# Four attention layers on one core: replicated bias rows, an epsilon tile, and a place of its own for every step of every group

## What is computed

```python
def _L0_xattn_ref(query, key, Wq, bq, Wk, bk, Wv, bv, Wo, bo):     # and the same once more as L3
    Q = query @ Wq + bq; K = key @ Wk + bk; V = key @ Wv + bv
    weights = softmax(Q @ K.T * scale)
    return query + (weights @ V) @ Wo + bo
def _L1_xattn_ref(text, audio, video, ...):                        # audio = ctx, video = side
    out_a, out_v = _cma(text, audio, ...), _cma(text, video, ...)  # layer norms, then attention
    output = out_a + out_v + text
    return _ln(output, ln_g, ln_b) @ fc_W + fc_b + output
def _L2_xattn_ref(emb, latent, ...):
    w = softmax(q @ k.T * scale, axis=1)                           # over the queries
    x = w @ v + emb
    return (x - mu) * rsqrt(var + EPS) * gamma + beta
```

## Time and profile before

| what | value |
|---|---|
| median of 3 runs | 614.36 us (613.43 to 615.67) |
| the profiled execution, its time | 613.34 us |
| its span in the trace | 611.5 us |
| mean granted clock of PE | 0.993 of full speed |
| PE busy, instructions | 582.3 us (95%), 4872 |
| DVE busy | 537.5 us (88%) |
| POOL busy | 520.0 us (85%) |
| ACT busy | 431.5 us (71%) |

### The profile page before, as it was taken

How to read it: one execution, slowest core, us unless ns; L and a number is a source line. 1 busy time by engine, 2 the same in 40 slices (tenths; PEclk the granted TensorE clock), 3 DMA queues, 4 the chain that set the end, 5 groups by cost and what they waited for, 6 DMA issues and landing times. The chain is left out here.

```text
span 611.5 us, 16892 instructions
## 1 busy us (share of the span) xinstructions
PE 582.3 (95%) x4872; PEld 567.7 (93%) x4872; DVE 537.5 (88%) x1685; ACT 431.5 (71%) x1473; POOL 520.0 (85%) x694
## 2 busy tenths in 40 slices
PE   4889999899999999999999999999999999999985
PEld 4778999899999999999999999999999899999974
DVE  1457789999999999999999999999999999989993
ACT  2546967777777778778777777877876788677443
POOL 3268887898999999999999999999999999867763
PEclk9998999999999999999999999999999999999999
DMA  8512211003222211122222221112333020000012
GB/s 274 217 62 70 82 48 46 3 1 96 80 78 80 78 56 51 54 80 79 78 80 79 79 79 53 48 60 78 114 104 114 17 89 28 18 3 19 19 35 70
DMA packets 28076, 42.80 MB, mean 70 GB/s; under 512 B 2513, under 2 KB 19793, under 8 KB 27985
## 3 DMA queue, kind: packets, MB, share of 16 engines
q1 hardware_dynamic: 27986, 41.72, 20.6%
HBM read 33.32 MB, written 8.39 MB: 68 GB/s over the span
## 5 line engine op out<-in xcount | busy, mean ns | idle before, releaser
L720 ACT ACTIVATE prob_L<-bank,neg_max_L 128x128 f32<-128x128 f32 x320 | 114.1, 379 | 70.1 <-DVE neg_max_L L952 69.7
L1082 POOL TENSOR_SCALAR xhat_ln<-x,rstd_ln,shift_ln 128x256 f32<-128x256 f32 x128 | 71.1, 564 | 14.0 <-issue 7.4
L652 ACT ACTIVATE oT_hi_L<-bank 128x256 fp32r<-128x256 f32 (+1 forms) x128 | 55.9, 460 | 34.4 <-PE bank L476 34.4
L720 ACT ACTIVATION_READ_ACCUMULATOR prob_L<-bank,neg_max_L 128x1 f32 x320 | 69.1, 216 | 0.0
L952 DVE TENSOR_REDUCE neg_max_L<-bank 128x2 f32<-128x256 f32 (+1 forms) x128 | 59.0, 477 | 11.5 <-PE bank L470 11.1
L652 ACT ACTIVATE xT_hi_L<-bank 128x512 fp32r<-128x512 f32 (+1 forms) x96 | 59.5, 620 | 7.4 <-PE bank L448 7.1
L854 DVE TENSOR_TENSOR oT_lo_L<-bank,oT_hi_L 128x256 fp32r<-128x256 f32 (+1 forms) x128 | 58.7, 478 | 2.9 <-ACT oT_hi_L L652 2.8
L1076 POOL TENSOR_TENSOR rstd_ln<-var_eps_ln,minus_half 128x2 f32<-128x2 f32 x64 | 45.3, 708 | 12.6 <-DVE var_eps_ln L919 7.4
L1116 POOL TENSOR_TENSOR xT_lo_L<-x_in,xT_hi_L 128x512 fp32r<-128x512 f32 x32 | 41.0, 1282 | 12.2 <-ACT xT_hi_L L652 12.2
L652 ACT ACTIVATE probT_L<-bank 128x256 f32<-128x256 f32 (+1 forms) x96 | 47.4, 495 | 4.3 <-PE bank L454 4.1
L985 DVE TENSOR_TENSOR x<-bank,x_bias 128x512 f32<-128x512 f32 x64 | 43.8, 685 | 6.5 <-PE bank L489 4.3
(11 more groups left out here) (217 smaller groups left out, 2390.9 us busy)
## 6 DMA issues: line engine op xcount, KB each, us to landing
x_in<-in_x SPq DMA_DIRECT2D x32, 512.0 KB, 4.2
ctx_in<-in_ctx SPq DMA_DIRECT2D x32, 256.0 KB, 4.3
out<-y SPq DMA_DIRECT2D x32, 256.0 KB, 2.2
side_in<-in_side SPq DMA_DIRECT2D x32, 128.0 KB, 2.5
WqT_L<-in_L_WqT SPq DMA_DIRECT2D x3, 256.0 KB, 4.3
Wo_L<-in_L_Wo SPq DMA_DIRECT2D x2, 256.0 KB, 4.7
WkT_L<-in_L_WkT SPq DMA_DIRECT2D x3, 128.0 KB, 4.1
WvT_L<-in_L_WvT SPq DMA_DIRECT2D x2, 128.0 KB, 4.0
```

The costliest lines, as they stand in the source:

```text
L652: activation(to, of, ACT.Copy).then_inc(done[step], 1)
L720: last = activation(at(prob[k], g)[:, b, :], block(bank, b), ACT.Exp, bias=at(neg_max[k], g)[:, b:b + 1], accum_out=at(total[k], g)[:, b:b ...
L1082: last = pool.tensor_scalar(at(to, g)[:, n, :], tile, at(rstd[k], g)[:, n:n + 1], at(shift[k], g)[:, n:n + 1], ALU.mult, ALU.add)
```

## The change

Four things.

1. The biases that were added on PE by a product of a row of ones with a bias row (`ones_row`, `row`) are gone. Ten rows of weights (`L0_bo`, `L1a_bo`, `L1v_bo`, `L3_bo`, `L3_b1`, `fc_bias`, `L2_bv`, `L3_g1` and the two key gains) are loaded by DMAs that write one row to all 128 partitions. They are added on DVE (`bias_plus`, which takes the place of an ACT copy) or multiplied in on POOL (`gained_L1a`, `gained_L1v`).
2. `var_eps` is a `tensor_tensor` with a tile `epsilon` in the place of a `tensor_scalar` with a number.
3. The preparations are cut into single steps (`M_L0`, `N_L0`, `m_L0`, ...), each with a place in the table, and the weights come in smaller loads with a semaphore each (`load_qk_`, `load_vo_`).
4. The table `STARTS` holds a number for every step and every group, 32 in a row, in the place of one pattern and the shifts `COMES`.

```diff
-STARTS = {"load_x": 0, "hi_L0": 107, "lo_L0": 281, "load_ctx": 580, "Q_L0": 626, "hi_ctx": 640, "q_L0": 727,
...
+    "rstd_keys": [2220, 2626, 2725, 4293, 5070, 6321, 7384, 8075, 8327, 12940, 13236, 15067, 16634, 17974, 20211, 21563, 23380,
...
-    table = [(STARTS[name] + COMES[g], g, name) for name in STARTS for g in range(GROUPS)]
...
+    table = [(times[g], g, name) for name, times in STARTS.items() for g in range(GROUPS)]
...
-        ones_row = sb("ones_row", [1, P])
...
+        epsilon = {e: sb(f"epsilon_{i}", [P, 2 * GROUP]) for i, e in enumerate((EPS_L1, EPS_L2))}
...
+            def replicated(to, r, what):
+                n, width = ROWS.index(r), to.shape[1]
+                sp.dma_start(to[:], ins["rows"][n:n + 1, 0:width].to_broadcast([P, width])).then_inc(weights[what], 16)
+
+            def load_qk(a):
+                return lambda: two(a, "WqT", "WkT", "qk")
...
-                dve.tensor_scalar(at(var_eps[k], g)[:], mv[:, :, 1], eps, None, ALU.add).then_inc(done[f"var_{k}"], 1)
+                if g == 0:
+                    prepared(dve, "constants")
+                dve.tensor_tensor(at(var_eps[k], g)[:], mv[:, :, 1], epsilon[eps][:, 0:len(tiles)], ALU.add).then_inc(done[f"var_{k}"], 1)
...
+            def bias_plus(key, to, use, added):
+                dve.tensor_tensor(to[:], bank_of(use)[:, 0:D], added[:], ALU.add).then_inc(done[key], 1)
...
+            def gained(a):
+                def of():
+                    pool.wait_ge(weights[f"{a}_qk"], TWO)
+                    pool.wait_ge(weights[f"gain_{a}"], ONE)
+                    w = stage[a]["WkT"]
+                    pool.tensor_tensor(w[:], w[:], gain[a][:].unsqueeze(1).to_broadcast([P, T, P]), ALU.mult).then_inc(done[f"gained_{a}"], 1)
+                return of
```

More of the change, by code:

```diff
@@ L61 @@
+PREPARATIONS = {"M_L0": 395, "N_L0": 615, "m_L0": 484, "n_L0": 528, "M_L1a": 1027, "N_L1a": 2128, "m_L1a": 1205, "M_L1v": 1116, "N_L1v":
[11 rows of a table added]
+COPIES = {"x_in": 3, "x_bias": 3, "x2_bias": 2, "token_sums": 2, "x3_bias": 2, "ctx_in": 10, "side_in": 3, "keys": 3, "keysT": 2,
[9 rows of a table added]
 SCALE = float(D) ** -0.5
@@ L77 @@
               "S_L3": "exp_L3", "PT_L3": "pT_L3", "O_L3": "oT_lo_L3", "OUT_L3": "out_L3"}
[L79 to L87, removed]
@@ L88 @@
-SMALL = [f"{what}_{k}" for what in ("stats", "mean", "var") for k in ("keys", "ln1", "lnf", "ln2")] + ["x_gamma"]
-SIGNALS = {"TensorE": {"keys_L1": ["gain_L1a", "gain_L1v"], "products_L0": ["M_L0", "N_L0"], "vectors_L0": ["m_L0", "n_L0"],
[13 rows of a table removed]
+EMPTIED_BY |= {"m_L0": "m_col_L0", "n_L0": "bias_L0", "m_L1a": "m_col_L1a", "m_L1v": "m_col_L1v", "n_L1": "bias_L1", "n_fc": "bias_fc",
+               "mean_fc": "centred_fc", "M_L2": "M_lo_L2", "k_L2": "k_bias2", "m_L3": "m_col_L3", "n_L3": "bias_L3"}
+EMPTIED_BY |= {f"{w}_{a}": f"{w}_lo_{a}" for w in "MN" for a in ATTENTIONS}
@@ new lines @@
+OF_ENGINE = {"TensorE": [f"{w}_{a}" for w in "MNm" for a in ATTENTIONS] + ["n_L0", "n_L1", "n_L3", "n_fc", "mean_fc", "M_L2", "k_L2"],
+             "ScalarE": ([f"{w}_hi_{a}" for w in "MN" for a in ATTENTIONS] + [f"M0_{a}" for a in ("L1a", "L1v", "L3")]
+                         + ["N0_L1a", "N0_L1v", "gained_fc", "F_hi", "M_hi_L2", "Wv2_hi"]),
+             "VectorE": (["scaled"] + [f"{w}_lo_{a}" for w in "MN" for a in ATTENTIONS] + [f"m_col_{a}" for a in ATTENTIONS]
+                         + ["bias_L0", "bias_L1", "bias_L3", "bias_fc", "centred_fc", "F_lo", "M_lo_L2", "k_bias2", "Wv2_lo"]),
+             "GpSimd": ["constants", "gained_L1a", "gained_L1v", "rows_L1", "rows_L3"] + [f"rep_{a}" for a in ATTENTIONS + ["fc"]]}
@@ L212, in build @@
             Wv2 = sb("Wv2", [P, D], where=staging)
-            rows = sb("rows", [1, len(ROWS), D], where=staging)
+            rows = {r: sb(f"row_{r}", [P, D], where=staging) for r in ("L0_bo", "L1a_bo", "L1v_bo", "L3_bo", "L3_b1", "fc_bias")}
+            gain = {a: sb(f"gain_{a}", [P, P], where=staging) for a in ("L1a", "L1v")}
             for a in ATTENTIONS + ["fc"]:
@@ L278, in col @@
             return of[:, n, t:t + 1]
-        def row(name, width=D):
-            return rows[0:1, ROWS.index(name), 0:width]
         def flat(tile):
@@ L413, in fc, with of @@
-            def fc():
-                pe.wait_ge(weights["fc"], FC_WEIGHTS)
+                def of():
+                    prepared(pe, "scaled")
+                    pe.wait_ge(weights[f"{a}_qk"], TWO)
+                    if a in LN_KEYS:
+                        prepared(pe, f"gained_{a}")
+                    bank = bank_for(pe, f"m_{a}")
+                    terms = [(stage[a]["WkT"][:, h, :], col(f"{a}_bq", h, scaled_cols)) for h in range(T)]
+                    if a in LN:
+                        prepared(pe, f"M0_{a}")
+                        terms += [(M0[a][:, t, :], col(f"{a}_b1", t, scaled_cols)) for t in range(T)]
+                    for n, (stationary, moving) in enumerate(terms):
+                        last = mm(bank[:, 0:1], stationary, moving, start=n == 0, stop=n == len(terms) - 1)
+                    last.then_inc(done[f"m_{a}"], 1)
@@ new lines, in query_bias, with output_bias, of @@
+                return of
+            def output_bias(key, attentions):
+                def of():
+                    bank = bank_for(pe, f"n_{key}")
+                    terms = []
+                    for a in attentions:
+                        prepared(pe, f"rep_{a}")
+                        pe.wait_ge(weights[f"{a}_vo"], TWO)
+                        terms += [(rep[a]["bv"][:, h, :], stage[a]["Wo"][:, h, :]) for h in range(T)]
+                        if a in LN_KEYS:
+                            prepared(pe, f"N0_{a}")
+                            terms += [(rep[a]["b2"][:], N0[a][:])]
+                    for n, (stationary, moving) in enumerate(terms):
+                        last = mm(bank[:, 0:D], stationary, moving, start=n == 0, stop=n == len(terms) - 1)
+                    last.then_inc(done[f"n_{key}"], 1)
+                return of
@@ L415, in fc, with n_fc @@
+            def n_fc():
+                pe.wait_ge(weights["fc"], ONE)
                 prepared(pe, "rep_fc")
                 bank = bank_for(pe, "n_fc")
-                terms = [(rep["fc"]["bv"][:, t, :], fcW[:, t, :]) for t in range(T)] + [(ones_row[:], row("fc_bias"))]
-                for n, (stationary, moving) in enumerate(terms):
-                    last = mm(bank[:, 0:D], stationary, moving, start=n == 0, stop=n == len(terms) - 1)
+                for t in range(T):
+                    last = mm(bank[:, 0:D], rep["fc"]["bv"][:, t, :], fcW[:, t, :], start=t == 0, stop=t == T - 1)
@@ L1067, in keys_L1, with replicated, of @@
-            def keys_L1():
-                replicated("L1a", "L1a_bv")
-                replicated("L1v", "L1v_bv")
+            def replicated(a):
+                def of():
+                    pool.wait_ge(weights["cols"], ONE)
+                    for t in range(T):
+                        last = pool.tensor_copy(rep[a]["bv"][:, t, :], col("fc_b" if a == "fc" else f"{a}_bv", t).to_broadcast([P, P]))
+                    if a in LN_KEYS:
+                        last = pool.tensor_copy(rep[a]["b2"][:], col(f"{a}_b2").to_broadcast([P, P]))
+                    last.then_inc(done[f"rep_{a}"], 1)
+                return of
```

349 lines of the change are left out of this document (185 added, 164 removed), and 213 rows, old and new, of tables (COPIES, PREPARATIONS, SIGNALS, STARTS).

## The result

The changed kernel takes 644.37 us (642.68 to 647.02, 4 runs) against 613.89 (613.01 to 615.67) on the same chip: a ratio of 1.048, interval 1.044 to 1.052. 598 had been forecast, with a tenth for slower. The profiled execution took 647.02 us, its span is 645.1.

What follows compares the result with a forecast made beforehand. PE was taken as the bound at 17.0 us per group, DVE close behind; 29.8 + 542.6 + 30.2 = 602.6 us of span, less 7.4 of waits, is 595.2, so 598 as median; range 589 to 608.

Steps and rivals of the forecast that it cites:

- The start: Up to PT_L0 of group 0: context issued at 16.5 us, landing at 22.2; PT_L0 at 29.8 against 33.91, 4.1 us earlier.
- the second rival: In the start, preparations run at PE's lower clock and give the gain back: 13 us more, 611 us, chance 0.13.
- All waits kept: Whole kernel, if every wait after the start stays: 29.8 + 542.6 + 30.2 = 602.6 us of span.
- the term of 542.6 us: After PT_L0 of group 0: PE's remaining 4726 instructions at 0.1148 us each.
- the 7.4 us taken off on top: Waits expected to go: 3.5 of 8.4 us in the filling, 3.9 of 7.8 in the middle, nothing in the tail.
- the 1.4 us for the missing products: In the filling: 14 PE instructions of 256 columns, at 0.215 instead of 0.115 us, are gone.
- half of the middle's waits would go: In the middle: the new order moves large POOL steps from rstd_ steps somewhat, saving 3.9 of 7.8 us.
- The epsilon edit: var_eps on DVE as tensor_tensor: still held behind POOL with two SBUF inputs, so priced at nothing.
- The order, the step that failed: In the middle: PE stays the bound at 17.0 us per group against DVE's 16.3; holds bind only over 2.2 us per group.
- the third rival: In the middle, the new order puts more DVE steps under POOL's; holds of 3.0 us per group: 622 us, chance 0.10.
- The count of neighbours: In the groups: 74 instead of 87 of 128 rstd_ steps right behind a large POOL step, so half the middle's waits go.
- The signs: Checks: PE 1730 to 1745 from 200 to 400 us; var_eps over 40 us; refuted under 1710 or by lower-clock preparations.

Runs made afterwards that it cites:

- e2: The changed kernel with every group step from 25 us of its table on put back into the old order: 606.82 us, ratio 0.989.
- e9: The changed kernel in its own order, with var_eps as a tensor_reduce with one SBUF input instead of a tensor_tensor: 620.45 us.
- e4: The changed kernel in its own order, with shift folded into POOL's normalisation (subtract, mult) and epsilon added on ACT: 725.07 us.
- e6: Epsilon added on ACT instead of DVE, in one of two orders: 642.04 us in the changed kernel's own order, 630.63 in the old order behind the new start.

## Why the prediction was wrong, step by step

**The start, right in kind, 2.3 us short.** PE of after in time, as in the earlier trace rows:

```profile
14.95 1.91 PE L547 MATMUL bank<-WkT_L1a,WqT_L1a 128*128 128x128 f32 x8
16.65 1.92 PE L547 MATMUL bank<-WkT_L1v,WqT_L1v 128*128 128x128 f32 x8
...
24.56 0.69 PE L660 MATMUL bank<-ctx_in,qT_L 128*128 128x128 f32 x4
25.08 1.06 PE L547 MATMUL bank<-WkT_L,WqT_L 128*128 128x128 f32 x8
...
32.13 0.38 PE L644 MATMUL bank<-ident,prob_L 128*128 128x128 f32 x2
```

On SP's list, where the earlier trace rows had 12.82:

```profile
17.35 0.43 SPq L517 DMA_DIRECT2D ctx_in<-in_ctx  x1
```

`ctx_in_0` is issued at 17.35 us (16.5 forecast), so a load that replicates a row costs SP no more than another. `M_L1a` begins at 14.95, 2 us later than worked out: POOL's wait for the input ended at 10.96 us and not at 9.6, and the six instructions of `Q_L0` (13.51 to 14.95), which stand ahead of it, were left out of the sum. It and `M_L1v` go 1.70 us from start to start where the same shape at 25.08 takes 0.90: PE had stood 4.09 us before `Q_L0`, and its granted clock is 0.50 from 15 to 18 us, the lower of its two levels, and 1.00 from 19 us on. So the second rival had it right for these steps, and not for all. From 14.95 us on PE has no wait, so the scores, at 24.56 instead of 22.2, waited for PE's own list and not for the context. `PT_L0` stands at 32.13, not 29.8, just outside the 28 to 32 that were named, as the issue at 17.35 is outside 16 to 17.

The second rival's price was also summed with two factors: 5.9 us ahead of the scores goes by 1.88 / 1.03, and 7.1 behind them by 2. With the first for both it is 12 us and not 13, 610 us.

**The filling and the middle.** "All waits kept" was 602.6 us of span; the run with the old order behind the new start has 604.4, so the term of 542.6 us and the count of instructions hold. Of the 7.4 us taken off on top nothing came: from 34 to 100 us that kernel does 511 PE instructions, before 502, 9 more or 1 us, which the 1.4 us for the missing products already cover. From 100 to 560 us it does 3940, before 3939. That half of the middle's waits would go had no mechanism behind it beyond a count of neighbours.

**The epsilon edit**, priced at nothing: 1.001. Right, and for the reason given.

**The order, the step that failed.** The prediction held that holds on DVE cost nothing while DVE's busy time fits into PE's. It asked whether PE stays the bound, and answered with busy times: DVE 16.3 us per group against PE's 17.0, so holds cost something only past 2.2 us per group. The holds were 2.4 (76 us over 32 groups, against 60 in the old order). By the third rival's own formula (the excess per group, over 30 groups) that is 0.2 x 30 = 6 us. Between the two orders it was 37.6. Its mechanism was right, and both its chance (0.10) and its price were wrong, since it took DVE for a vessel that fills. By PE's waits, what counts is what stands behind a held step. The new order has fewer microseconds of holds in `var_eps` than the old (43 against 51), and they cost 23.9 us instead of 5.7. The holds also lie elsewhere; `var_eps_ln` of e2, the old order (minimum, median, maximum in ns):

```profile
L1164 DVE TENSOR_TENSOR var_eps_ln<-mean_var_ln,epsilon x64: 160/653/1376, 38.7 to 587.3; 128x2 f32<-128x2 f32 x64
```

and of after:

```profile
L1135 DVE TENSOR_TENSOR var_eps_ln<-mean_var_ln,epsilon x64: 160/198/1486, 39.4 to 627.6; 128x2 f32<-128x2 f32 x64
```

In this group the old order is held in more than half of its instances, and the new one less often; with `var_eps_keys` and `var_eps_lnf` it is the other way round (medians of 557 and 272 ns after, 300 and 161 in e2). PE waits 4.3 us in all from 100 to 560 us in the old order and 30 in the new. My reading is that the repeated pattern has room behind its held step, and that a table that places each step by readiness has none, as at 295 us above. That the cost depends on the order is shown; how much room each place has was not measured.

**The count of neighbours** (74 instead of 87 `rstd_` behind a large POOL step) looked at `rstd_` on POOL. The held instructions are on DVE, among them `shift_` and `x3_bias`, and these were not counted: their holds are 18 and 15 us, where the old order has 7 and 2.

**The signs.** PE's count under 1710 in 200 us, 1559, was named as what would refute the forecast; so was the lower clock in the preparations, which came for two of them. `var_eps` in sum, 63.4 us, stayed over the 40 that were to confirm it, with maxima over 1 us, and so misled: a sum of durations doesn't see who waits.

## What to carry to other kernels

An order is as good as the durations it was made for: before placing steps by readiness, list the instructions whose time depends on what another engine does, and look for each at what stands behind it in its list. Better still, take away the dependence by another form of the same step; that was worth 24 us in the tight order and 6 in the loose one. When all engines are less busy and the kernel is slower, look at the lists and not for a bound. Leaving out a tenth of one engine's work tells in one run whether that engine sets the time; its busy share didn't here.

## What the runs showed of the hardware

- DVE behind POOL: a `tensor_tensor` of 128x2 with two SBUF inputs takes 160 to 1486 ns (after); the same sum as a `tensor_reduce` 156 to 160 in 64 instructions (e9).
- POOL's `tensor_scalar` on 128x256 f32 takes 558 ns in the median with (mult, add) (after) and 1220 with (subtract, mult) (e4); on 128x128, 452 and 794.
- An activation of 128x2 with a bias out of SBUF took 295 ns on ACT in the median (e6), nearly twice what DVE's `tensor_reduce` takes for the same sum (157).
- In after, the ten DMAs that replicate one row to 128 partitions were issued in 0.43 to 0.58 us each but for one of 1.23, as the loads of weights beside them (0.42 to 0.94).
